# One squaring pass and one VectorE sum per block, and messages read in place by TensorE, in a graph layer with residual and layer norm

## The reference, cut to what matters

```python
row, col = src, dst                                   # 50,000 edges, dst sorted
msg = jnp.concatenate([x[row], edge_attr], axis=1)    # 64 + 32 features
msg = msg @ W1 + b1                                   # 96 -> 128
agg = jax.ops.segment_sum(msg, col, num_segments=100000)
out = jnp.concatenate([x, agg], axis=1) @ W2 + b2     # 64 + 128 -> 64
x = layernorm(x + out)                                # over 64 features, eps 1e-5
```

## Time and profile before

| | before |
|---|---|
| median of 3 runs | 1054.15 us |
| span of the profiled execution | 801.0 us |
| PE busy | 615.5 us, 77% |
| DVE busy | 522.7 us, 65% |
| ACT busy | 398.6 us, 50% |
| POOL busy | 423.9 us, 53% |
| mean granted TensorE clock | 0.843 of full |

### The profile page before, as it was taken

One profiled execution on the slowest core, in us unless ns is written; L12 is line 12 of the kernel. 1 busy time (PEld: TensorE's weight loads), 2 busy tenths in 40 slices (PEclk: granted clock), 3 DMA queues, 4 the chain that ended last, 5 costly groups with the idle time before them and its releaser, 6 DMA issues. The chain is left out here.

```text
span 801.0 us, 29016 instructions
## 1 busy us (share of the span) xinstructions
PE 615.5 (77%) x8418; PEld 544.4 (68%) x8419; DVE 522.7 (65%) x1826; ACT 398.6 (50%) x2012; POOL 423.9 (53%) x514
## 2 busy tenths in 40 slices
PE   1345445677778888888898898989898888878785
PEld 1344435566767777777777787878777777768675
DVE  3670111354465648858887788788787787878876
ACT  0011122102234344444567777777777777757655
POOL 5676766711676766475467777767466445200000
PEclk9655555657688779979999999999999999989988
DMA  2121222200223233333345545555455455533432
GB/s 63 28 37 36 37 37 34 57 9 12 61 54 82 59 86 79 79 78 79 100 110 139 127 122 139 129 136 147 115 139 144 110 132 134 134 86 115 126 97 81
DMA packets 168753, 71.47 MB, mean 89 GB/s; under 512 B 61570, under 2 KB 162447, under 8 KB 168720
## 3 DMA queue, kind: packets, MB, share of 16 engines
q1 hardware_dynamic: 104592, 51.74, 22.7%
q0 software_dynamic: 12544, 12.87, 8.5%
q10 hardware_dynamic: 51584, 6.41, 5.1%
HBM read 45.37 MB, written 25.60 MB: 89 GB/s over the span
## 5 line engine op out<-in xcount | busy, mean ns | idle before, releaser
L363 POOL DMA_INDIRECT feat<-in_x,src_now x392 | 393.6, 1004 | 255.4 <-issue 94.6
L775 DVE TENSOR_SCALAR onehot<-node_of_col,group_base,dst_of 128x256 bf16<-128x256 bf16 x952 | 287.4, 348 | 106.1 <-issue 78.9
L473 PEld LDWEIGHTS ps_y<-z_window,onehot 128*128 128x128 bf16 x5712 | 202.6, 101 | 65.8 <-DVE z_window L778 46.0
L473 PE MATMUL ps_y<-z_window,onehot 128*128 128x64 bf16 x5712 | 226.7, 198 | 26.6 <-DVE z_window L778 23.5
L574 ACT ACTIVATE square<-ps_y 128x64 bf16<-128x64 f32 x784 | 162.7, 239 | 135.8 <-PE ps_y L464 133.2
L574 ACT ACTIVATION_READ_ACCUMULATOR square<-ps_y 128x1 f32 x784 | 159.5, 224 | 0.0
L539 ACT ACTIVATE feat_t<-ps_t 97x512 f32<-97x512 f32 x98 | 58.6, 598 | 179.8 <-PE ps_z L400 159.9
L400 PE MATMUL ps_z<-wz,feat_t 97*128 97x64 f32 x784 | 123.1, 324 | 24.6 <-DVE z_rest L700 24.5
L400 PEld LDWEIGHTS ps_z<-wz,feat_t 97*128 97x128 f32 x784 | 118.0, 238 | 33.2 <-DVE z_rest L700 31.8
L392 PE MATMUL ps_t<-ident,feat 128*97 128x128 f32 x392 | 72.3, 333 | 86.8 <-DMA feat<-in_x,src_now 63.7
L464 PE MATMUL ps_y<-wx,x_t 128*128 128x128 f32 x784 | 118.4, 296 | 13.1 <-issue 8.7
(11 more groups left out here) (107 smaller groups left out, 226.2 us busy)
## 6 DMA issues: line engine op xcount, KB each, us to landing
xin<-in_x SPq DMA_DIRECT2D x97, 256.0 KB
out<-yout SPq DMA_DIRECT2D x97, 256.0 KB
feat<-in_x,src_now POOLq DMA_INDIRECT x392
feat<-in_edge_attr ACTq DMA_DIRECT2D x97, 64.0 KB
z<-in_src SPq DMA_DIRECT2D x1, 192.0 KB
z<-in_dst SPq DMA_DIRECT2D x1, 192.0 KB
xin<-in_x SPq DMA_DIRECT2D x1, 128.0 KB
out<-yout SPq DMA_DIRECT2D x1, 128.0 KB
```

The lines of the kernel that those rows point to most:

```text
L363: nc.gpsimd.indirect_dma_start(out=feat[h][:, half * CB + c, 0:C], out_offset=None, in_=x[:, :], in_offset=bass.IndirectOffsetOnAxis(ap=sr ...
L473: mm = nc.tensor.matmul(ps_y[h][:, col:col + C], onehot[h][:, g, s, a, :], z_window[h][:, g, s, part * C:(part + 1) * C], start=False, sto ...
L775: ins = nc.vector.tensor_scalar(onehot[h][:, g, s, :, :], node_of_col[:, :, :], base, dst_of[:, bass.ds(firsts[g] + (at + s), 1)], ALU.add ...
```

## The change

It does three things. ScalarE squares a whole block in one activation (128 x 512, float32 out); VectorE adds it up with one `tensor_reduce` a block, in a new step `sums` at the head of the next unit, and ScalarE takes the root of unit u-1 inside unit u. `z_window`, its copies and its semaphores are gone; L473's matmuls read `z` at register addresses. TensorE waits for `z_kept` before the units of a round. GpSimd clears `square` at the start, two memsets.

```diff
-        z_window = [sb(f"z_window{h}", [P, G, 2, 3 * C], bf16) for h in range(2)]
-        square = [sb(f"square{h}", [P, G * A, C], bf16) for h in range(2)]
+        chunk_order = [sb(f"chunk_order{h}", [P, CHUNKS]) for h in range(2)]
+        square = [sb(f"square{h}", [P, G * A, C]) for h in range(2)]
...
+            for h in range(2):
+                nc.gpsimd.memset(square[h][:, :, :], 0.0).then_inc(s_const, 1)
...
             def block_sum(k, h):
-                _, (second, third) = load_steps(mybir.EngineType.PE, b, G, 2, G * CHUNKS // 2)
+                _, (*firsts, second, third) = load_steps(mybir.EngineType.PE, b, 0, G + 2, G * CHUNKS // 2)
...
-                def pair_sum(g):
+                def pair_sum(g, at):
                     for s in range(2):
                         for a in range(A):
                             col = (g * A + a) * C
                             for part in range(3):
                                 mm = nc.tensor.matmul(ps_y[h][:, col:col + C], onehot[h][:, g, s, a, :],
-                                                      z_window[h][:, g, s, part * C:(part + 1) * C], start=False, stop=False)
+                                                      z[:, firsts[g] + (at + s), part, :], start=False, stop=False)
                 for g in range(G):
-                    pe.wait_ge(window_ready, G * b + g + 1)
                     pe.wait_ge(hot_ready, G * b + g + 1)
-                    pair_sum(g).then_inc(group_summed, 1)
+                    pair_sum(g, 0).then_inc(group_summed, 1)
                 with pe.If(second > 0):
                     for g in range(G):
...
-                        pe.wait_ge(window2_ready, turn_no)
                         pe.wait_ge(hot2_ready, turn_no)
-                        pair_sum(g)
+                        pair_sum(g, 2)
                     with pe.If(third > 0):
-                        _, firsts = load_steps(mybir.EngineType.PE, b, 0, G, CHUNKS - 4)
...
                 edge_round(k)
-                for_units(pe, mybir.EngineType.PE, k - LAG, unit)
+                units_of_round = read_units(mybir.EngineType.PE, k - LAG)
+                pe.wait_ge(z_kept, k - LAG)
+                run_units(pe, *units_of_round, unit)
...
             def keep_y(u, h):
                 act.wait_ge(y_done[h], u + 2)
-                act.wait_ge(squared[h], u + 1)
-                act.wait_ge(s_root, u + 1)
-                for q in range(G * A):
-                    sq = nc.scalar.activation(square[h][:, q, :], ps_y[h][:, q * C:(q + 1) * C], ACT.Square,
-                                              accum_out=sumsq[:, h, q:q + 1])
-                sq.then_inc(squared[h], 1)
+                act.wait_ge(summed[h], u + 1)
+                nc.scalar.activation(square[h][:, :, :], ps_y[h][:, :].rearrange("p (n c) -> p n c", c=C),
+                                     ACT.Square).then_inc(squared[h], 1)
...
             def root(u):
                 for h in range(2):
-                    act.wait_ge(squared[h], u + 2)
-                act.wait_ge(s_rstd, u + 2)
+                    act.wait_ge(summed[h], u + 1)
+                act.wait_ge(s_rstd, u + 1)
...
             def unit(u):
                 for h in range(2):
                     keep_x(u, h)
+                root(u)
                 for h in range(2):
                     keep_y(u, h)
-                root(u)
...
+            def sums(u):
+                for h in range(2):
+                    dve.wait_ge(squared[h], u + 1)
+                    nc.vector.tensor_reduce(sumsq[:, h, :], square[h][:, :, :], AX.X, ALU.add).then_inc(summed[h], 1)
+
             def unit(u):
+                sums(u)
                 one_hots(u, 0)
                 one_hots(u, 1)
                 normalize(u)
```

More of the change, by code:

```diff
@@ L134, in gnn_residual_layernorm @@
         below, holds = (buf[:, 0:CHUNKS] for buf in x_t)
-        chunk_up, chunk_down = (
-            buf[:, :, :, :].rearrange("p g s q -> p (g s q)").bitcast(f32)[:, 0:CHUNKS] for buf in z_window)
+        chunk_up, chunk_down = (buf[:, :] for buf in chunk_order)
         score, least_row, most_row = (
@@ L179, in gnn_residual_layernorm @@
         hot_ready = sem("onehot_ready")
-        window_ready = sem("z_window_ready")
         group_summed = sem("group_summed")
         hot2_ready = sem("onehot_of_second_pair_ready")
-        window2_ready = sem("z_window_of_second_pair_ready")
         hotx_ready = sem2("onehot_x_ready")
@@ L188, in gnn_residual_layernorm @@
         squared = sem2("squared")
+        summed = sem2("squares_summed")
         s_root = sem("std_ready")
@@ L418, in _ @@
             pe.wait_ge(s_wload, 16 * 8)
-            pe.wait_ge(s_const, 12)
+            pe.wait_ge(s_const, 14)
             nc.tensor.transpose(ps_a[0:H, 0:F], w1aug[:, :], ident[0:F, 0:F]).then_inc(s_w, 1)
@@ L456, in block_sum @@
                 b = 2 * k + h
-                _, (second, third) = load_steps(mybir.EngineType.PE, b, G, 2, G * CHUNKS // 2)
+                _, (*firsts, second, third) = load_steps(mybir.EngineType.PE, b, 0, G + 2, G * CHUNKS // 2)
+                firsts = [nc.s_assert_within(f, 0, CHUNKS - 4, skip_runtime_bounds_check_because="so the table is made")
+                          for f in firsts]
                 pe.wait_ge(y_kept[h], k + 1)
@@ L525, in _ @@
                 edge_round(k)
-                for_units(pe, mybir.EngineType.PE, k - LAG, unit)
+                units_of_round = read_units(mybir.EngineType.PE, k - LAG)
+                pe.wait_ge(z_kept, k - LAG)
+                run_units(pe, *units_of_round, unit)
             edge_round(PAIRS - 1, loads=2)
+            pe.wait_ge(z_kept, PAIRS - 1 - LAG)
             for_units(pe, mybir.EngineType.PE, PAIRS - 1 - LAG, unit)
@@ L590, in unit @@
                     keep_x(u, h)
+                root(u)
                 for h in range(2):
                     keep_y(u, h)
-                root(u)
-            act.sem_inc(s_root)
             for h in range(2):
@@ L602, in _ @@
                 load_ea(0, h)
-            act.wait_ge(s_const, 12)
+            act.wait_ge(s_const, 14)
             nc.scalar.activation(std_eps[:, :], eps[:, :], ACT.Sqrt)
@@ L644, in _ @@
                 for_units(act, mybir.EngineType.Activation, k - LAG, unit)
+            root(PAIRS)
         @block.vector
@@ L669, in _ @@
             dve.wait_ge(s_w, 2)
-            dve.wait_ge(s_const, 12)
+            dve.wait_ge(s_const, 14)
             link(nc.vector.tensor_copy(wz[:, :], ps_z[0:F, 0:C]))
@@ L770, in one_hots, with pair @@
                 dve.wait_ge(hots_used[h], k + 1)
-                def pair(g, at, hot, window):
+                def pair(g, at, hot):
                     base = group_base[:, bass.ds(b * G + g, 1)]
@@ L777, in pair @@
                     ins.then_inc(hot, 1)
-                    nc.vector.tensor_copy(z_window[h][:, g, :, :],
-                                          z[:, bass.ds(firsts[g] + at, 2), :, :].rearrange("p s q c -> p s (q c)")
-                                          ).then_inc(window, 1)
                 for g in range(G):
-                    pair(g, 0, hot_ready, window_ready)
+                    pair(g, 0, hot_ready)
                 with dve.If(second > 0):
@@ L786, in one_hots @@
                         dve.wait_ge(group_summed, G * b + g + 1)
-                        pair(g, 2, hot2_ready, window2_ready)
+                        pair(g, 2, hot2_ready)
                     with dve.If(third > 0):
@@ L834, in _ @@
             for_units(dve, mybir.EngineType.DVE, PAIRS, unit)
+            sums(PAIRS)
             normalize(PAIRS)
```

## The result

| | before | after |
|---|---|---|
| median of 3 runs | 1054.15 us | 1258.51 us (1258.38 to 1260.82) |
| ratio | | 1.192, 95% interval 1.187 to 1.198 |
| span of the traced execution | 801.0 us | 1256.6 us |
| PE / DVE / ACT busy | 616 / 523 / 399 us | 903 / 512 / 286 us |
| mean granted clock | 0.843 | 0.749 |

The change makes the kernel slower by 204 us. The forecast was slower, 1186 us, with 1115 to 1270 as the range.

A forecast was written before the change was run, and what follows sets the result against it. VectorE was taken to pace units that follow a unit (8.2 us), TensorE those in rounds (10.8 us). Stage increases of +59, +22, +3, +38 and +10 for the clock gave +132, so 1186 us, range 1115 to 1270.

The forecast's parts named there:

- Rivals 1 and 3: First: TensorE's queue hides addresses, about 1063 us, chance 0.07; third: VectorE's dropped copies are the gain, 1021 us, chance 0.03.
- the queue's depth: TensorE's queue of 64 entries: addresses could be worked out far ahead, and a group would stay at 0.39 us.
- The sum: Whole kernel: 12.4 us for every unit, stage increases and clock added, +132 us in all, a span of 933 us.
- the addresses queue up behind from 2.75 on: TensorE in a round with edge work: busy till 3.8 us after the last dense matmul, addresses prepared meanwhile from 2.75.
- its +59: Third stage, units 9 to 39: 31 units at 12.4 us make 384 us, against 325.7 before.
- Units 1 to 8: Second stage: 16 pairs a unit at 0.15 us more, plus read and first pairs, less `z_rest` waits: +22 us.
- The last nine: Final units and output: nine at 12.4 us plus 18 us of stalls and output, 130 us, so +38.
- unit 0: First unit, mostly the unchanged loop of line 504: 16 pairs at +0.15 us, so +3 us.
- The clock: TensorE idles and feeds matmuls at half rate, so some float32 work runs at the lower level: +10 us.
- Rival 2: TensorE's clock falls to 1.2 GHz for most float32 work: +100 us on top, 1230 to 1275 us, chance 0.10.
- Parts 2 to 4: VectorE's copies against reductions: net nothing; wait for squares: first pair 2.75 us after last dense matmul; ScalarE and start: nothing.
- 253.2 us lie around the span: Outside the profiled span: a 253.2 us difference to the median, carried unchanged onto the predicted span of 933 us.

The follow-up runs named there:

- the squares alone: Kernel before with one square a block and VectorE's sums at the head of the next unit, windows and fixed addresses kept: 844.4 us, ratio 1.051.
- the addresses alone: Kernel before with windows and their copies replaced by register addresses, squares and accumulators as before: 1039.0 us, ratio 1.295.
- the sums later: Changed kernel with VectorE's sums moved between the one-hots of the two blocks: 1032.6 us, ratio 1.288.

## Why the prediction was right, and where it was short

**Direction and mechanism: right.** The address operations pace TensorE's pairs. Rows 8 and 9 gave 0.13 us for a matmul with a new address and 0.03 for one without, and that is what line 475 does: 2856 operations of 46 ns at the median, six a pair, and a pair of 0.84 to 0.92 us where I took 0.83. Constant addresses take the whole loss away where there are no gaps, and twelve a pair bring nearly the step that the price says. Rivals 1 and 3 (hidden, faster) fall with that, and so does the queue's depth as a way out: it helps only where the sequencer isn't held up by something else, as the run with early reads shows.

**The term mis-sized: what a unit in a round takes.** The sum had 12.4 us for every unit, with or without a round before it. Where a unit follows a unit this holds: from the end of the last dense matmul, at 568.8 us, to the first pair 2.5 us pass (forecast 2.75), 0.74 of them idle, and the median of these units is 12.9 us:

```profile
568.60 1.78 PE L451 MATMUL ps_x<-ident,xin 128*128 128x128 f32 x8
570.22 0.38 PE L462 MATMUL ps_y<-b2rows,ones_bf 65*128 65x512 bf16 x1
571.33 3.67 PE L475 MATMUL ps_y<-z,onehot 128*128 x48 [0.74 <-DVE onehot L775]
```

With a round before it, it is 14.4 us in the round shown (539.16 to 553.53 above) and 15.05 at the median of the third stage: 3.83 + 3.35 + 2.10 + 3.59 + 1.50 against 2.75 + 3.32 + 1.75 + 3.32 + 1.30. The step that failed is "the addresses queue up behind from 2.75 on". The first pair starts only 3.83 us in, after transposes and bias, and its matmuls are as slow as later ones: the sequencer itself is held up, by the two reads of the tables and the branches between the messages and the first pair, and has no lead. The other excess is the read between the blocks, 1.47 us and not 0.82, and 0.34 us of branches at the loop's end. Rounds longer than the one shown have a read of up to 1.85 us or a dense part at the lower clock level, 2.07 us instead of 1.16. Of the 71 us by which the third stage exceeds its +59, 23 rounds x 2.6 are 60 and 8 units x 0.5 are 4; the remaining 7 are not assigned.

**Units 1 to 8: +42, not +22.** I charged 0.15 us a pair, from 0.68 to 0.83, as if VectorE had set the pace in all sixteen. Their 128 pairs took 76 us before, 0.59 a pair (4.4 us for the eight of a first block, 5.3 for those of a second), and 112 us after, 0.87 a pair. That is +36 where 0.15 a pair gave +19. The error was to treat the pace seen in the row as the one that the other pairs had too.

**The last nine: +49, not +38**, and unit 0 +4, not +3: small misses, which were not traced further.

**The clock.** +10 us was taken. The dense part alone is busy for 39 us more than with constant addresses (1.22 us a block grew to 1.62), at 0.88 of the full clock in the third stage against 0.98; how much of the 39 us is on the path isn't shown. Rival 2 put the time at 1230 to 1275 us, and 1258.5 lies in that range, but the clock did not bring it there: 1258.5 holds the gaps, which both kernels have, and of the 224 us that constant addresses take away the pairs cover 201. Its own working doesn't hold either, as 5.5 x 40 x 0.7 is 154 us and not 100. Its reason, idle time, is also not what the trace shows: TensorE is busy for 93% of the third stage at 0.88, where before it was busy for 90% at 0.98. With constant addresses the clock is back, so it is pairs fed at half the rate that go with the lower one.

**Parts 2 to 4.** Reductions 0.683 us each: right. The net on VectorE was taken as nothing, and the run that tests it, the one with constant addresses, bears this out in sum: 803.6 against 801.5 us, with 0.9 us lost in units that follow a unit and 0.7 won in rounds. The +42 us of the squares alone are not that net, since the copies stay there. Whether the squares cost anything with the addresses in isn't settled by 1039.0 against 1027.7 us, as the table reads differ by 22 us between the two traces.

**The sum and what lay around it.** Without gaps the span rose by 221 us (803.8 to 1025.3), where the sum had +132: the result lies in the range by its width, not by the point, and near its upper end. The step "253.2 us lie around the span" was wrong; about 2 us do. It did little harm only by luck, because the gaps cost both kernels about the same.

## What to carry to other kernels

Count the register operations that stand between small matmuls: here each new address took 0.12 to 0.13 us of TensorE's sequencer, and a matmul of 64 columns with its weight load 0.03, so one address to two matmuls more than halves the rate (0.87 against 0.39 us a pair) and one to four already shows (0.57). Where addresses can't be avoided, let nothing that the sequencer must wait for stand right before them: with the table reads moved ahead the second block's four pairs took 2.43 us instead of 3.59. A copy to a fixed place on an engine that works beside TensorE (0.16 us of VectorE for a pair) is cheaper than six addresses (0.5 us of TensorE). And when a span and the times don't agree to a few microseconds, that is a finding to be cleared up before anything is summed on it.

## What the runs showed of the hardware that was not expected

The same program ran at 802 us on two chips and at 1029 on a third, every time. In the traces with the longer times there are gaps of about 0.73 us and its multiples before TensorE's matmuls, in straight code without a wait. In the changed kernel's they lie in 30 of the 34 blocks that come right after edge work and in one of the 64 others, and begin most often after the 27th matmul; with three addresses and with none also mostly after the 24th to 28th, with twelve after the 19th to 24th or the 31st to 35th. That looks like a sequencer that waits for its own instructions. The Trainium skill (Runtime: NRT & Kernel Launch, section "Instruction fetch mechanics") has instructions streamed in blocks of 16 KiB with the cost mostly hidden. The trace agrees on the size, 20 transfers of 0.33 MB in all on this queue:

```profile
q8 instruction: 20, 0.33, 0.1%
```

But such a transfer is not what the gaps wait for: between 202 and 1113 us, where 236 gaps of over 0.3 us lie, the trace has no instruction transfer on any queue, and from 1114 us on, where this queue has 14, these gaps are missing. So the cause is open, and 96 more instructions in the loop brought none of it on a chip without it.

A table read on TensorE takes 0.55 us for two values and 0.83 for six, so 0.07 a value; but for a unit's second block the same six take 1.47 us, at either clock level and with register or constant addresses. It isn't the place between two blocks that does it: with the reads moved ahead, the second stands right behind the first, and in all 49 units they take 0.82 and 1.47 us. With two values the second block's read is no longer than the first's. The two reads differ in their place in the code and in the part of the table they take, and neither was varied. In the runs with the addresses alone and with the sums later, many of these reads take 2.0 to 2.6 us. What adds the 0.64 us, and what adds the rest, is open.
